# First self attention of a decoder on one Trainium2 core: the output product in rounded halves, one batch later, with the next scores ahead of the weighting of values

## The reference, cut to what matters

```python
q = (x @ Wq.T).reshape(Bv, Tv, H, D)          # H, D = 8, 128
k = (x @ Wk.T).reshape(Bv, Tv, 1, D)
v = (x @ Wv.T).reshape(Bv, Tv, 1, D)
k = k + sinusoidal_pe(1, D, k.dtype)
...
q = q + sinusoidal_pe(Tv, D, q.dtype)[None, None]
scores = jnp.einsum('bhtd,bsd->bhts', q, k1) * scale
scores = jnp.where(causal[None, None], scores, jnp.finfo(scores.dtype).min)
probs = jax.nn.softmax(scores, axis=-1)
attn = jnp.einsum('bhts,bsd->bhtd', probs, v1)
out = jnp.transpose(attn, (0, 2, 1, 3)).reshape(Bv, Tv, H * D)
return out @ Wo.T
...
x = x + _L0_attn_ref(_layernorm(x, axis=-1), L0_attn_Wq, L0_attn_Wk, L0_attn_Wv, L0_attn_Wo)
```

## Time and profile before

| | |
|---|---|
| median of 3 runs | 1724.64 us (1720.76 to 1724.7) |
| the profiled execution: time, span | 1724.28 us, 1722.4 us |
| PE busy | 1632.5 us, 95% of the span |
| PEld busy | 1313.1 us, 76% |
| DVE, ACT, POOL busy | 1084.2 us (63%), 776.1 us (45%), 544.8 us (32%) |
| mean granted TensorE clock | 0.983 |
| projections of group 2 to those of group 3 | 44.4 to 58.4 us, to 77.2 us |
| batch loop | 77.2 to 198.5 us |

### The profile page before, as it was taken

One profiled execution on the slowest core, in us unless ns is written; L12 is line 12 of the kernel. 1 busy time (PEld: TensorE's weight loads), 2 busy tenths in 40 slices (PEclk: granted clock), 3 DMA queues, 4 the chain that ended last, 5 costly groups with the idle time before them and its releaser, 6 DMA issues. The chain is left out here.

```text
span 1722.4 us, 33298 instructions
## 1 busy us (share of the span) xinstructions
PE 1632.5 (95%) x11494; PEld 1313.1 (76%) x11494; DVE 1084.2 (63%) x2543; ACT 776.1 (45%) x2178; POOL 544.8 (32%) x581
## 2 busy tenths in 40 slices
PE   6999899999999999999999988899988899988998
PEld 6877678778778878777887866799977777655666
DVE  5566467666777666667676664455354578856664
ACT  2356354444454455454545441365402577743211
POOL 1022223333333333333333334244430033354000
PEclk9999999999999999999999999899998999998999
DMA  3100300000000000000001004575310000010000
GB/s 102 48 11 1 117 12 11 11 10 10 0 10 10 10 10 10 8 2 10 10 10 55 11 2 167 140 255 191 104 64 21 25 2 2 2 60 1 11 11 22
DMA packets 48808, 67.46 MB, mean 39 GB/s; under 512 B 11826, under 2 KB 42770, under 8 KB 46034
## 3 DMA queue, kind: packets, MB, share of 16 engines
q1 hardware_dynamic: 47186, 62.66, 11.6%
q0 software_dynamic: 1536, 3.67, 0.7%
HBM read 57.02 MB, written 9.31 MB: 39 GB/s over the span
## 5 line engine op out<-in xcount | busy, mean ns | idle before, releaser
L709 POOL TENSOR_TENSOR l0x_p<-l0x_p,l0x_inv 112x488 f32<-112x488 f32 x256 | 261.7, 1043 | 426.4 <-DVE l0x_inv L806 425.2
L934 ACT ACTIVATE l0x_p<-l0x_s,l0x_low 112x488 f32<-112x488 f32 x256 | 177.9, 696 | 255.3 <-DVE l0x_low L795 222.6
L795 DVE CUSTOM_DVE_ANT_0 l0x_s<-l0x_score_ps,l0x_bias 112x488 f32<-112x488 f32 x256 | 160.2, 664 | 95.0 <-PE l0x_score_ps L1081 85.7
L1102 PE MATMUL l0x_oT_ps<-l0x_pT,l0x_v 122*64 122x112 f32 x2048 | 127.2, 266 | 7.0 <-ACT l0x_pT L940 6.1
L1089 PEld LDWEIGHTS l0x_pT_ps<-ident,l0x_p 112*122 112x122 f32 x1024 | 99.0, 138 | 45.3 <-issue 39.2
L1102 PEld LDWEIGHTS l0x_oT_ps<-l0x_pT,l0x_v 122*64 122x64 f32 x2048 | 99.6, 137 | 42.5 <-issue 31.8
L1089 PE MATMUL l0x_pT_ps<-ident,l0x_p 112*122 112x112 f32 x1024 | 126.1, 266 | 0.4 <-POOL l0x_p L709 0.3
L782 DVE TENSOR_TENSOR l0x_kT_lo<-l0x_proj_ps,l0x_kT_hi 128x488 fp32r<-128x488 f32 x128 | 84.1, 667 | 63.2 <-ACT l0x_kT_hi L924 63.2
L1037 PE MATMUL l0x_proj_ps<-l0x_kvT_hi,l0x_wkv_hi 128*128 128x488 f32 x256 | 104.7, 409 | 2.9 <-DVE l0x_kvT_lo L770 2.9
L1046 PE MATMUL l0x_proj_ps<-l0x_wkv_hi,l0x_kvT_hi 128*122 128x512 f32 x256 | 105.2, 411 | 0.0
L1047 PE MATMUL l0x_proj_ps<-l0x_wkv_lo,l0x_kvT_hi 128*122 128x512 f32 x256 | 101.0, 395 | 0.0
(11 more groups left out here) (392 smaller groups left out, 4045.6 us busy)
## 6 DMA issues: line engine op xcount, KB each, us to landing
l0f_w<-in_l0f_w SPq DMA_DIRECT2D x21, 1024.0 KB
l0x_c_in<-in_ctx SPq DMA_DIRECT2D x16, 375.0 KB
l1x_gram_context<-in_ctx SPq DMA_DIRECT2D x16, 375.0 KB
sorted_x<-l0x_zeros SPq DMA_DIRECT2D x1, 2816.0 KB, 15.3
l0f_xs<-sorted_x SPq DMA_DIRECT2D x21, 128.0 KB, 2.2
sorted_y<-l0f_z SPq DMA_DIRECT2D x21, 128.0 KB, 1.8
l0x_wkv<-in_l0x_wkv SPq DMA_DIRECT2D x2, 1024.0 KB, 9.2
x<-in_x SPq DMA_DIRECT2D x4, 448.0 KB, 7.8
```

What stands on the lines that cost most here:

```text
L709: nc.gpsimd.tensor_tensor(p[:, i % 2, a, :], p[:, i % 2, a, :], inv[:, i % 2, a:a + 1].broadcast_to([S, KEYS]), ALU.mult).then_inc(pn_read ...
L795: nc.vector.tensor_tensor_reduce(s_sb[:, h % 2, :], score_ps[0:S, h % 2, 0:KEYS], bias[:], -SCALE, 3.4e38, ALU.add, ALU.min, low[:, h:h + ...
L934: nc.scalar.activation(p[:, h // 2 % 2, h % 2, :], s_sb[:, h % 2, :], ACT.Exp, scale=-1.0, bias=low[:, h:h + 1], accum_out=total[:, h:h + ...
L1102: done = nc.tensor.matmul(oT_ps[a * DH:(a + 1) * DH, 0, (i % 4) * S:(i % 4 + 1) * S], v[:, t, (2 * i + a) * DH:(2 * i + a + 1) * DH], pT[: ...
```

## The change

The output product of `project_out` is made of rounded operands in three products (`oT_hi` by `wo_hi`, `oT_hi` by `wo_lo`, `oT_lo` by `wo_hi`), 24 matmuls a batch instead of 8, and all of it stands a batch later, behind `transpose_p(b + 1)`. ScalarE takes each half of `o_ps` out rounded (`round_o`), VectorE makes the remainder of each half (`split_o`), and both tiles are single. `score(b + 2)` comes ahead of `weigh_values(b)`, whose halves wait one by one. `softmax` is cut in `add_mask` and `find_shift`: VectorE's order in the loop is mask(b + 2), remainder of half 0, maximum and shift of b + 2, remainder of half 1. The output weights are rounded by ScalarE in four parts after `take_inputs(3)`, and their remainders are made by VectorE after heads 4 to 7 of group 2. The diff, without the names of the new semaphores:

```diff
--- before.py
+++ after.py
@@ -131,12 +131,13 @@
     mv, half, rstd, rstd2 = norms
     with ExitStack() as ctx:
         ph = Phase(nc, ctx, "l0a")
-        wo = ph.sb("wo", [128, H, D])
+        wo_hi, wo_lo = ph.sb("wo_hi", [128, H, D], F32R), ph.sb("wo_lo", [128, H, D], F32R)
         pos_q, pos_k = ph.sb("pos_q", [DH, S]), ph.sb("pos_k", [DH, 1])
         causal = ph.sb("causal", [S, S])
         rvar = ph.sb("rvar", [S, B])
         qT, kT, v = ph.sb("qT", [DH, H, B * S]), ph.sb("kT", [DH, B * S]), ph.sb("v", [S, B, DH])
-        pT, oT = ph.sb("pT", [S, H, S]), ph.sb("oT", [DH, 2, H, S])
+        pT = ph.sb("pT", [S, H, S])
+        oT_hi, oT_lo = ph.sb("oT_hi", [DH, H, S], F32R), ph.sb("oT_lo", [DH, H, S], F32R)
         p, pn = ph.sb("p", [S, 2, H, S]), ph.sb("pn", [S, 2, H, S])
         top, shift = ph.sb("top", [S, 2, H]), ph.sb("shift", [S, 2, H])
         total, inv = ph.sb("total", [S, 2, H]), ph.sb("inv", [S, 2, H])
@@ -187,7 +190,7 @@
                                         start=True, stop=True)
             done.then_inc(score_done, 1)
 
-        def softmax(dve, b):
+        def add_mask(dve, b):
             j = b % 2
             dve.wait_ge(score_done, b + 1)
             since(dve, pn_ready, b - 1)
@@ -195,6 +198,9 @@
                 p[:, j].rearrange("p (a h) s -> p a h s", a=2),
                 score_ps[0:S, 2 * j:2 * j + 2, 0:4 * S].rearrange("p a (h s) -> p a h s", h=4),
                 causal[:, None, None, :].broadcast_to([S, 2, 4, S]), ALU.add).then_inc(softmax_step, 1)
+
+        def find_shift(dve, b):
+            j = b % 2
             dve.wait_ge(softmax_step, b * 4 + 1)
             nc.vector.tensor_reduce(top[:, j], p[:, j], AX.X, ALU.max).then_inc(softmax_step, 1)
             dve.wait_ge(softmax_step, b * 4 + 2)
@@ -223,6 +229,7 @@
             wq, wk, wv = (ph_in.sb("wq", [128, KC, H * DH]), ph_in.sb("wk", [128, KC, DH]),
                           ph_in.sb("wv", [128, KC, DH]))
             wq_hi, wq_lo = ph_in.sb("wq_hi", [128, KC, H * DH], F32R), ph_in.sb("wq_lo", [128, KC, H * DH], F32R)
+            wo = ph_in.sb("wo", [128, H, D])
             xn, xT = ph_in.sb("xn", [S, QB, D]), ph_in.sb("xT", [128, 2, KC, QT])
             xT_hi, xT_lo = ph_in.sb("xT_hi", [128, 2, KC, QT], F32R), ph_in.sb("xT_lo", [128, 2, KC, QT], F32R)
             block = projections.enter_context(nc.Block())
@@ -313,12 +320,18 @@
                             qT[:, i, q * QT:(q + 1) * QT].rearrange("p (j t) -> p j t", j=QB),
                             query_bank(i).rearrange("p (j t) -> p j t", j=QB),
                             pos_q[:, None, :].broadcast_to([DH, QB, S]), ALU.add).then_inc(dve_step, 1)
+                        if q == Q - 2 and i >= 4:
+                            part = slice(2 * i - 8, 2 * i - 6)
+                            dve.wait_ge(wo_hi_ready, i - 3)
+                            nc.vector.tensor_tensor(wo_lo[:, part], wo[:, part], wo_hi[:, part].bitcast(F32), ALU.subtract
+                                                    ).then_inc(wo_lo_ready, 1)
                         if q == Q - 1 and i == 1:
-                            dve.wait_ge(late_w, 32)
-                            softmax(dve, 0)
+                            add_mask(dve, 0)
+                            find_shift(dve, 0)
                         elif q == Q - 1 and i == 5:
                             invert_sums(dve, 0)
-                softmax(dve, 1)
+                add_mask(dve, 1)
+                find_shift(dve, 1)
 
             @block.scalar
             def _(act):
@@ -345,6 +358,11 @@
                         take_inputs(q + 1)
                     else:
                         exp(act, 0)
+                    if q == Q - 2:
+                        act.wait_ge(late_w, 32)
+                        for n in range(4):
+                            nc.scalar.activation(wo_hi[:, 2 * n:2 * n + 2], wo[:, 2 * n:2 * n + 2], ACT.Copy
+                                                 ).then_inc(wo_hi_ready, 1)
                     act.wait_ge(proj_done, 9 * q + 9)
                     nc.scalar.activation(kT[:, q * QT:(q + 1) * QT], o_ps[:, 0, 0:QT], ACT.Identity, bias=pos_k[:, 0:1])
                     nc.scalar.activation(v[:, q * QB:(q + 1) * QB, :].rearrange("p j d -> p (j d)"),
@@ -439,6 +457,13 @@
                         nc.vector.tensor_copy(pT[:, 4 * a:4 * a + 4, :].rearrange("p h s -> p (h s)"),
                                               score_ps[0:S, 2 * (b % 2) + a, 0:4 * S]).then_inc(pT_ready, 1)
 
+                def split_o(b, a):
+                    dve.wait_ge(oT_hi_ready, b * 2 + a + 1)
+                    heads = slice(4 * a, 4 * a + 4)
+                    nc.vector.tensor_tensor(oT_lo[:, heads, :].rearrange("p h s -> p (h s)"), o_ps[:, a, 0:4 * S],
+                                            oT_hi[:, heads, :].rearrange("p h s -> p (h s)").bitcast(F32), ALU.subtract
+                                            ).then_inc(oT_lo_ready, 1)
+
                 def update(b):
                     dve.wait_ge(y_done, b + 1)
                     update_row(nc, dve, x, stats, y_ps[0:S, b % 2, 0:D], b, x_step)
@@ -455,12 +480,16 @@
                         update(b - 1)
                     if b + 1 < B:
                         invert_sums(dve, b + 1)
+                    if b + 2 < B:
+                        add_mask(dve, b + 2)
+                    split_o(b, 0)
+                    if b + 2 < B:
+                        find_shift(dve, b + 2)
+                    split_o(b, 1)
                     if b == B - 2:
                         dve.wait_ge(x_step, 2 * BULK)
                         for done_b in range(BULK):
                             nc.vector.bn_aggr(mv[:, done_b, :], stats[:, done_b, :]).then_inc(mv_step, 1)
-                    if b + 2 < B:
-                        softmax(dve, b + 2)
                     if b in (5, 7, 9, 11):
                         split_next((b - 5) // 2)
                     if b == 7:
@@ -479,16 +508,17 @@
 
             @block.scalar
             def _(act):
-                def copy_o(b):
-                    act.wait_ge(o_done, b + 1)
-                    since(act, y_done, b - 1)
-                    nc.scalar.activation(oT[:, b % 2].rearrange("p (a h) s -> p a (h s)", a=2), o_ps[:, :, 0:4 * S],
-                                         ACT.Copy).then_inc(o_ready, 1)
+                def round_o(b, a):
+                    act.wait_ge(o_done, b * 2 + a + 1)
+                    since(act, y_done, b)
+                    nc.scalar.activation(oT_hi[:, 4 * a:4 * a + 4].rearrange("p h s -> p (h s)"), o_ps[:, a, 0:4 * S],
+                                         ACT.Copy).then_inc(oT_hi_ready, 1)
 
                 for b in range(B):
                     if b + 1 < B:
                         exp(act, b + 1)
-                    copy_o(b)
+                    round_o(b, 0)
+                    round_o(b, 1)
                     if b in (5, 7, 9, 11):
                         act.wait_ge(next_w_w, 48)
                         c, part = w.PARTS[(b - 5) // 2]
@@ -506,32 +536,32 @@
                             done.then_inc(pT_done, 1)
 
                 def weigh_values(b):
-                    since(pe, o_ready, b)
                     for a in range(2):
+                        since(pe, oT_lo_ready, 2 * (b - 1) + a + 1)
                         pe.wait_ge(pT_ready, b * 2 + a + 1)
-                        done = nc.tensor.matmul(o_ps[:, a, 0:4 * S], v[:, b, :], pT[:, 4 * a:4 * a + 4, :],
-                                                start=True, stop=True)
-                    done.then_inc(o_done, 1)
-
-                def project_out(b, part):
-                    if part == 0:
-                        pe.wait_ge(o_ready, b + 1)
-                        since(pe, x_step, b * 2 - 3)
-                    for c in range(4 * part, 4 * part + 4):
-                        done = nc.tensor.matmul(y_ps[0:S, b % 2, 0:D], oT[:, b % 2, c, :], wo[:, c, :],
-                                                start=(c == 0), stop=(c == H - 1))
-                    if part == 1:
-                        done.then_inc(y_done, 1)
+                        nc.tensor.matmul(o_ps[:, a, 0:4 * S], v[:, b, :], pT[:, 4 * a:4 * a + 4, :],
+                                         start=True, stop=True).then_inc(o_done, 1)
+
+                def project_out(b):
+                    pe.wait_ge(wo_lo_ready, 4)
+                    since(pe, x_step, b * 2 - 3)
+                    y = y_ps[0:S, b % 2, 0:D]
+                    for c in range(H):
+                        if c % 4 == 0:
+                            pe.wait_ge(oT_lo_ready, b * 2 + c // 4 + 1)
+                        nc.tensor.matmul(y, oT_hi[:, c, :], wo_hi[:, c, :], start=(c == 0), stop=False)
+                        nc.tensor.matmul(y, oT_hi[:, c, :], wo_lo[:, c, :], start=False, stop=False)
+                        done = nc.tensor.matmul(y, oT_lo[:, c, :], wo_hi[:, c, :], start=False, stop=(c == H - 1))
```

(12 more changed lines are left out.)

## The result

| | before | after |
|---|---|---|
| median | 1725.32 us (8 runs, 1720.76 to 1728.2) | 1734.78 us (8 runs, 1729.42 to 1740.14) |
| ratio, 95% interval | | 1.0061 [1.0046, 1.0076] |
| profiled execution: time, span | 1724.28, 1722.4 us | 1738.47, 1736.6 us |
| mean granted clock | 0.983 | 0.977 |

The change costs 9.5 us by the medians. I had 5.4 us and a range that ended at 1734.5, 0.3 us short of this median.

The account below looks back on a forecast made before the run. TensorE's own work was taken to bound the kernel, busy for 95% of the span. A pause of +6.3, a low clock of +2.3 and a loop gain of -3.2 made +5.4 us, so 1730.0 us, range 1725.5 to 1734.5.

Parts of the forecast that it names:

- Part 1: Projection group 2: VectorE waits for the late rounding of the output weights, leaving TensorE idle 6.3 us.
- Part 2: Behind the pause in group 2: TensorE runs at half clock, costing 2.3 us, bounds 0 to 3.0.
- The rival in which the clock holds: Behind the pause: TensorE stays at 2.4 GHz, so only +3.1 us, 1727.7; chance 0.10.
- Part 3: Batch loop: TensorE waits for the second remainder, period 6.99 us, loop 118.0 us, a gain of 3.2 us.
- the chain: Batch loop: scores, mask, rounding, remainder, maximum, shift, second remainder, second half of output product; a period of 6.99 us.
- loaded batches: Four loop batches where VectorE also works for the next stage: 0.82 twice, 2.02 and 1.79 us beyond 6.99.
- own work: Batch loop: remainder comes in time, loop runs at TensorE's 6.66 us, gain 7.5, total +1.1, 1725.7; chance 0.10.
- gains nothing: Batch loop: VectorE or starts after waits cost 0.3 us more a batch, period 7.3, total 1733.5; chance 0.15.
- Sum: Whole kernel: pause +6.3, clock +2.3, loop -3.2 make +5.4 us, 1730.0 us.
- Wrong: Signs against the forecast: keys at 55, clock 1.00 at 62, periods 6.7 or 7.3, or another stage longer through a 5 us shift.

Follow-up runs that it names:

- e2: Changed kernel, but VectorE makes the four remainders of the output weights in group 3 instead of group 2: 1726.26 us, ratio 1.0016 to before.
- e3: Kernel before plus the change's rounding and remainders of the output weights in group 2, read by nobody: 1732.36 us, ratio 1.0073 to before.
- e1: The changed kernel measured a second time, no edit: 1732.02 us, ratio 1.0055 to before.
- e13: e3 with the filler matmuls in the last batch of the cross attention: ratio 1.0034 to before.
- e10: Changed kernel plus filler matmuls of 128x384 in the cross attention's last batch: 1731.05 us, ratio 1.0034 to before.
- e6: Changed kernel plus 28 unused matmuls of 128x448 on TensorE in the pause of group 2: 1733.55 us, ratio 1.0048 to before.
- e15: e6 with the filler matmuls in the last batch of the cross attention: 1730.32 us, ratio 1.0013 to before.
- e4: Kernel before plus 16 dummy statistics at VectorE's very start, shifting all the rest in time: 1728.78 us, ratio 1.0033 to before.
- e9: Kernel before plus filler matmuls of 128x384 in the cross attention's last batch: 1722.42 us, ratio 0.9991 to before.
- e11: e7 plus filler matmuls of 128x384 in the cross attention's last batch: 1719.63 us, ratio 0.9973 to before.
- e16: e11 plus four matmuls of 128x512 between the loop's first transposes and third scores: ratio 0.9957 to before.
- e7: e2 with all products by oT_hi ahead of those by oT_lo: 1731.18 us, ratio 1.002 to before.
- e12: The kernel of e7 measured a second time, no edit: 1730.72 us, ratio 1.0027 to before.
- e5: e2 with the maximum and shift ahead of both remainders on VectorE: 1732.04 us, ratio 1.0034 to before.

## Why the prediction was wrong

**Part 1, the pause: right.** Keys at 61.68 against 55.15; 0.44 us of that is an offset of the whole execution (the keys of group 1 are as much later), and 6.09 is the pause. I had 6.3: the keys at 61.43 and the order of who waits for whom as in the profile. (The lower bound of 5.9 was added up wrong; its own rows give 6.1.) e2 took it away, and e3 made it alone.

**Part 2, the clock behind it: right in kind, and low.** The first transposes came 9.02 us later, 0.44 offset and 6.09 pause, so 2.49 for the clock (I had 2.3). The stretch was 6.8 us in four of the profiles with this pause and nothing in it (after, e1, e3, e13), and 10.2 in e10. The length alone doesn't give the cost: from the keys to T0, which is 22.10 at full clock, it is 24.6 in after, 24.7 in e1 and e3, and 25.1 in both e13 and e10, whose longer stretch began inside the pause. So it costs 2.5 to 3.0. With filler in the pause e6 has 22.10 again; by the ratios of e10 and e15 the filler is worth 3.6, give or take 3.3. The rival in which the clock holds fell. The page that I cited, "TensorE: Matmul & The Clock Gate" of the Trainium skill (Part 1, "What's actually happening"), had throttled as the default and activity as what releases it; the trace agrees with 0.50 behind the pause.

**Part 3, the loop: the chain was right to 0.03 us in each step, the gain put 0.5 too high.** Period 7.02 (6.99), loaded batches 0.78, 1.98, 0.78 and 1.76 beyond it (0.82, 2.02, 0.82, 1.79), loop 118.55 (118.0), gain 2.65 (3.2). The rivals "own work" and "gains nothing" both fell. What the sum didn't have is the clock at the loop's start: four of seven times the gain is 1.0 to 1.3 and not 2.65. I had priced the waits there as waits and not as a way to lose the clock.

**The sum: the failed step.** By rows, the first self attention costs 6.09 + 2.49 - 2.65 = 5.9 us, where I had 5.4, so nearly all that the argument spoke of came as forecast. The measurement is 9.5 (8.5 for the repeat by its medians, 9.5 by its ratio). The step that failed is the silent one in "Sum" and in the range: that every other stage, and the loop's edges, keep their time, so that an error can come only from the terms. I had it only as a last clause under "Wrong". It isn't the shift in time that I suspected there, since e4 was as late and paid it only once.

What the runs show in its place begins with the stages of the profiles, each from its first product on TensorE to that of the next stage, the first from the start of the span and the last to its end:

| us | before | after | e1 |
|---|---|---|---|
| first self attention | 199.4 | 205.8 | 206.2 |
| cross attention | 838.7 | 838.9 | 838.8 |
| experts of layer 0 | 264.3 | 273.7 | 264.5 |
| second self attention | 215.8 | 216.3 | 216.4 |
| second cross attention | 66.6 | 65.2 | 66.7 |
| feed-forward of layer 1 | 137.5 | 136.8 | 137.4 |

The windows of the experts' stage in before, after and e1, each to the microsecond:

```profile
1038.00:1302.00 264.00, 238.95 (x1698) 224.10 (x1698) 137.70 (x354) 94.79 (x252) 105.48 (x147) 0.97 0.47 150
1044.00:1318.00 274.00, 241.63 (x1698) 226.28 (x1698) 138.89 (x356) 95.10 (x252) 105.63 (x147) 0.94 0.46 145
1045.00:1309.00 264.00, 240.81 (x1698) 225.70 (x1698) 137.15 (x354) 94.97 (x252) 105.38 (x147) 0.95 0.48 150
```

This stage didn't keep its time, and not only here. In the five profiles with the old loop (before, e3, e4, e9, e13) it took 263.0 to 264.7 us; in the thirteen with the new one 264.1 to 273.7, eleven of them above 265, with a median of 266.6. In it the clock was at 0.50 for 13.7 to 20.5 us with the old loop, and for 11.3 to 30.7, with a median of 21.7, with the new one; TensorE was idle for 25 to 27 us and for 24 to 32. That is 2 to 3 us, the size of what is missing. It was seen only afterwards, in one profile of each kernel, the waits that grew aren't the same ones from profile to profile, and no run tests it, so that the change causes it isn't shown.

The clock is the other part: its low stretches fall in more places than I had charged. The span times what the mean clock lacks of 1 bounds what it took: 29 us in the profile before (0.017 of 1722.4), 40 in the one after (0.023 of 1736.6). The loop's start takes 1.3 to 1.5 us in some executions, the stretch behind the pause up to 0.5 more than in the profile after, and with the filler, which keeps the end of the cross attention out of it, +7.4 by the ratios and +8.6 by the medians is measured.

What stays open: 7.4 and 9.5 differ by less than their intervals, and where the 1.5 to 3.6 us beyond the 5.9 lie isn't settled. The end of the cross attention isn't their place in the two profiles of the change: the clock in the window 990:1060 was 0.88 in after and 0.90 in e1, 0.98 in before, but the stage took no longer. The experts' stage is the candidate that no run tests.

## What to carry to other kernels

A wait put in an engine's queue is paid by all that stands behind it: four remainders that nobody needed for another 30 us (they were done at 62.2, the first output product started at 92) cost 6 us of TensorE, and 2.5 to 3.0 more of its clock. Moving them by one group took the pause and its low clock away. The rounded product, with its products by `oT_hi` first, is then faster than the kernel before, once a few dummy products hold the clock at the end of the cross attention (e11, 0.9973; e16, 0.9957). When a local gain that the trace confirms doesn't arrive in the total, compare the granted clock in windows of every later stage before looking for another wait; and compare several executions, as one profile can hold a stretch that the next doesn't. One repeat that looks clean isn't enough to clear a stage either.

## What the runs showed of the hardware

- At one place, with the same instructions and the same wait of 1.08 us, the clock stayed in the kernel before and fell in e7, for stretches of 20.5 and 13.7 us. Of the 24 runs of e7's kernel (e7, e12) 13 had the mean clock of 0.975 or less that goes with it in the profiles of e5, e6 and e7; e12's own profile, at 0.977, had the 20.5 us too. TensorE was busy for 32.81 of the 37 us from 1003 to 1040 in e7, and without a gap from 1005.55 to 1029.69, of which the clock was 0.50 from 1006.0 to 1026.5:

```profile
1003.00:1040.00 37.00, 32.81 (x222) 28.01 (x220) 15.70 (x36) 12.10 (x30) 7.98 (x8) 0.59 0.00 0
```

  In e9, with the filler there, the same window has 32.77 us of work at a clock of 1.00, so the busy share in the row didn't tell which clock it ran at. Eight matmuls of 8 columns (L1162) took 1.66 us there against 0.95.
- The four matmuls of 128x384 took 0.96 us and cut the wait ahead of the weighting from 1.08 to 0.35 us; the kernel with them wasn't slower (0.9991), so work in this wait cost nothing that can be measured, and the clock in the window 1003:1040 was 1.00 (0.95 in before).
- A rounded matmul of 128x256 took 0.117 us from start to start in the new loop too, so 24 of them 2.81 us, as the earlier trace rows gave it.
